# First attention of a language-model tower: value products of two key tiles issued as one group, and the rows of -1 of three key buffers written by POOL

## What is computed

```python
h = _L0_tok_ref(x, ...)                                  # token + position embedding
h = h + _L0_attn_ref(_layernorm(h), W_Q, W_K, W_V, W_O)  # this attention
h = h + _L0_ffn_ref(...); h = h + _L1_attn_ref(...); h = h + _L1_ffn_ref(...)

# inside _L0_attn_ref
scores = jnp.einsum('bhsd,bhtd->bhst', Q, K) / jnp.sqrt(jnp.float32(D_K))
scores = jnp.where(causal[None, None], scores, -jnp.inf)
attn = jax.nn.softmax(scores, axis=-1)
out = jnp.einsum('bhst,bhtd->bhsd', attn, V)
```

## Time and profile before

| | |
|---|---|
| median of 3 runs | 1530.04 us (1529.1 to 1531.93) |
| the profiled execution, device time | 1528.33 us |
| its span, first to last instruction | 1526.6 us |
| first attention (`attend_pairs`) in the span | from 117.4 to about 463 us |
| a step of it in the middle, TensorE | 10.3 us, 28 steps of this kind (u = 4 to 31) |
| a step at its end, without A (u = 32 to 34) | 7.19 us |
| mean granted clock of TensorE | 0.917 |

### The profile page before, as it was taken

One profiled execution on the slowest core, in us unless ns is written; L12 is line 12 of the kernel. 1 busy time (PEld: TensorE's weight loads), 2 busy tenths in 40 slices (PEclk: granted clock), 3 DMA queues, 4 the chain that ended last, 5 costly groups with the idle time before them and its releaser, 6 DMA issues. The chain is left out here.

```text
span 1526.6 us, 31400 instructions
## 1 busy us (share of the span) xinstructions
PE 1291.8 (85%) x10719; PEld 1003.0 (66%) x10720; DVE 855.6 (56%) x1797; ACT 662.8 (43%) x1260; POOL 633.0 (41%) x569
## 2 busy tenths in 40 slices
PE   6878999999996968980899566689959999989996
PEld 3655555555555847770667455589958888878886
DVE  5997776776744966996555355454423333323332
ACT  3871555555563644440344344233313343333332
POOL 7865665565004220777200000067213454444553
PEclk9995999999998997785899878799979999999998
DMA  1678877767400004654443311011036435454331
GB/s 52 199 254 266 265 228 247 231 223 230 115 4 15 1 5 137 183 178 127 91 110 85 110 42 47 10 28 28 29 129 213 116 51 133 127 132 130 52 55 19
DMA packets 122872, 179.38 MB, mean 118 GB/s; under 512 B 26052, under 2 KB 83820, under 8 KB 122772
## 3 DMA queue, kind: packets, MB, share of 16 engines
q1 hardware_dynamic: 94212, 117.15, 25.5%
q0 software_dynamic: 28560, 60.91, 15.2%
HBM read 104.73 MB, written 74.31 MB: 117 GB/s over the span
## 5 line engine op out<-in xcount | busy, mean ns | idle before, releaser
L1574 DVE TENSOR_REDUCE att_top<-att_psS 128x4 f32<-128x512 f32 (+2 forms) x192 | 195.9, 1036 | 80.6 <-PE att_psS L1458 80.6
L2725 POOL DMA_INDIRECT out<-ffn1c_y,ffn1c_table x72 | 113.9, 1582 | 177.1 <-ACT ffn1c_y L2838 99.3
L2866 DVE TENSOR_TENSOR ffn1c_hid<-ffn1c_psG,ffn1c_sil 128x512 f32<-128x512 f32 x72 | 49.8, 692 | 144.3 <-PE ffn1c_psG L2766 144.3
L1545 ACT ACTIVATE att_prob<-att_psS 128x1024 f32<-128x1024 f32 (+1 forms) x96 | 84.6, 883 | 92.0 <-PE att_psS L1478 91.9
L1545 ACT ACTIVATE pairs_part<-att_psS 128x1024 f32<-128x1024 f32 (+1 forms) x96 | 84.5, 883 | 67.0 <-PE att_psS L1478 66.7
L1452 PE MATMUL att_psS<-pairs_ka,pairs_qa 48*128 48x384 f32 (+3 forms) x512 | 107.3, 429 | 5.8 <-PEq L198 4.0
L1472 PE MATMUL att_psS<-pairs_qa,pairs_ka 50*128 50x256 f32 (+3 forms) x512 | 99.5, 401 | 12.2 <-DVE att_top L1574 12.0
L2766 PE MATMUL ffn1c_psG<-ffn1c_w_h,ffn1c_xh 128*128 x288 | 97.8, 422 | 11.3 <-DMA ffn1c_w_l<-experts_lo 3.9
L2714 POOL DMA_INDIRECT ffn1c_rows<-normed_rows,ffn1c_table x72 | 71.0, 986 | 78.4 <-DVE ffn1c_gate L2886 53.7
L1452 PEld LDWEIGHTS att_psS<-pairs_ka,pairs_qa 48*128 48x128 f32 x512 | 52.2, 200 | 70.4 <-issue 47.5
L2766 PE MATMUL ffn1c_psG<-ffn1c_w_l,ffn1c_xh 128*128 x288 | 90.9, 397 | 0.0
(11 more groups left out here) (413 smaller groups left out, 3605.2 us busy)
## 6 DMA issues: line engine op xcount, KB each, us to landing
prep_raw<-in_w_all POOLq DMA_DIRECT2D x27, 512.0 KB, 4.6
experts_hi<-prep_hi POOLq DMA_DIRECT2D x27, 512.0 KB, 3.8
experts_lo<-prep_lo POOLq DMA_DIRECT2D x27, 512.0 KB, 6.1
ffn1c_w_h<-experts_hi SPq DMA_DIRECT2D x8, 1536.0 KB, 6.6
ffn1c_w_l<-experts_lo SPq DMA_DIRECT2D x8, 1536.0 KB, 10.9
qkv_near<-near_keys SPq DMA_DIRECT2D x32, 320.0 KB, 4.3
q_parts<-pairs_part SPq DMA_DIRECT2D x8, 1024.0 KB, 4.1
k_parts<-pairs_part SPq DMA_DIRECT2D x16, 512.0 KB, 6.0
```

The lines of the kernel that those rows point to most:

```text
L1545: act.activation(dst, src, ACT.Exp, scale=0.25).then_inc(s["exp"], 1)
L1574: dve.tensor_reduce(dst, src, AX.X, ALU.max).then_inc(s["max"], 1)
L2725: pool.indirect_dma_start(out=rows_out, in_=y[:, t.buf, :], in_offset=None, out_offset=bass.IndirectOffsetOnAxis(ap=table[:, t.value:t.val ...
L2866: dve.tensor_tensor(hid[:, t.par, :], psG[:, t.par, 1, :], sil[:, t.par, :], ALU.mult).then_inc(s["act"], 1)
```

## The change

Two edits. In TensorE's walk, V0 moves from n = 4 to n = 5, directly ahead of V1, and V2 moves from n = 0 to n = 1, directly ahead of V3. The matmuls are the same. And the three memsets of key buffers 3 to 5 leave VectorE's steps 1 to 3; POOL issues them at the head of its part of `attend_pairs`, ahead of the first piece.

```diff
-    def dve_minus_rows(self, dve, at):
-        dve.memset(self.ka[:, at].bitcast(F32), -1.0).then_inc(self.s_minus, 1)
+    def minus_rows(self, eng, at):
+        eng.memset(self.ka[:, at].bitcast(F32), -1.0).then_inc(self.s_minus, 1)
...
             for at in range(pairs.EARLY):
-                pairs.dve_minus_rows(dve, at)
+                pairs.minus_rows(dve, at)
...
             piece, n_pieces = split
+            for at in range(pairs.EARLY, LOADED):
+                pairs.minus_rows(pool, at)
             for u in range(n_pieces):
...
-                    if n >= 4 and 0 <= u - 3 < NU:
-                        values(u - 3, n - 4)
-                    if n <= 1 and 0 <= u - 4 < NU:
-                        values(u - 4, n + 2)
+                    if n == 5 and 0 <= u - 3 < NU:
+                        values(u - 3, 0)
+                        values(u - 3, 1)
+                    if n == 1 and 0 <= u - 4 < NU:
+                        values(u - 4, 2)
+                        values(u - 4, 3)
...
             for u in range(NU + 4):
-                if pairs.EARLY <= u + AHEAD < LOADED:
-                    pairs.dve_minus_rows(dve, u + AHEAD)
                 for n in range(6):
```

## The result

The changed kernel took 1524.9 us (median of 8, 1520.96 to 1527.02), the kernel before 1530.8 in the same sessions: ratio 0.9957, 95% interval 0.9936 to 0.9978. So the two ratios say 0.4 and 0.2% faster, and both intervals leave out 1; 1526.5 had been forecast.

The account below looks back on a forecast made before the run. TensorE is 96% busy in the middle, but its step is partly a loop through DVE, which bounds the first steps. Steps 1.7, steps without A 1.0 and start 0.8 make 3.5 us: 1526.5 against 1530.04, 8-in-10 range 1522 to 1530.5.

Parts of the forecast that it names:

- The walk: Middle attention step followed row by row from A0 with spacings of the earlier trace: 10.24 us instead of 10.30.
- The two loops through VectorE: Middle step: B3 waits for the maximum of A2, and B5, in the new order, for that of A4.
- The 0.66 wait ahead of B5: Middle step: without V0 ahead of it, TensorE reaches B5 at 7.28 and waits for DVE until 7.94.
- the merges' 0.64: TensorE work removed per middle step: two merges at 0.32 each (entry 0.14, join 0.18); 18 us over 28 steps.
- The term of the steps, 1.7 us,: Middle steps: 0.06 us saved in each of 28 steps, 1.7 us; bounds 0 to 3.4.
- The steps without A, 1.0 us,: Steps 32 to 34: first merge worth nothing, second counts, 3 x 0.32 = 1.0 us; bounds nothing and 1.9.
- The start, 0.8 us,: First steps: 1.0 us from moving the memsets off DVE, less 0.2 for a later clock rise.
- The 0.2 taken off for a later rise: Start: V0 of unit 0 begins later, so the clock may rise later; costs 0.2 us, bounds 0 and 1.7.
- Rival 1: Whole kernel: no visible change, step keeps 10.30 and the start's gain is lost; 1528 to 1531 us, chance 0.31.
- Rival 2: Middle steps: merges won in full on TensorE, half being 9 us; 1511 to 1521 us, chance 0.05.
- Rival 3: Middle steps: clock falls because of waits at B3 and B5; ten steps at 1.2 GHz give 1550, chance 0.05.
- Rival 4: Middle steps: join not won, step 10.42 (1531.6 us) or 10.60 (1536.6 us); chance 0.05.

Follow-up runs that it names:

- e2: Changed kernel with only V2 and V3 merged, V0 back between B4 and A5, memsets on POOL; ratio 0.9930 to the kernel before.
- e3: Changed kernel with only V0 and V1 merged, V2 and V3 apart as before, memsets on POOL; ratio 1.0032 to the kernel before.
- e4: Changed kernel with merged V0 and V1 issued between A5 and B5 instead of behind B5; 1509.61 us, ratio 0.9846 to the kernel before.
- e7: Changed kernel with POOL's splitting of the expert weights started three steps later; ratio 0.9961 to the kernel before.
- e8: e4 and e7 together, against the changed kernel; 1509.06 us, ratio 0.9859 to the kernel before.
- e9: The changed kernel itself, nothing altered, timed again on a third chip; 1604.56 us, ratio 0.9980 to the kernel before.
- e10: The version of e4 timed again on the same chip as e9; 1586.03 us, ratio 0.9869 to the kernel before.
- e5: The kernel of e1 run again for a profile (memsets on POOL, value groups apart); no ratio on record, profile span 1525.8 us.
- e6: Changed kernel with merged value groups but the three memsets back on VectorE; ratio 0.9996 to the kernel before.
- e1: Changed kernel with the value groups apart as before, so only the memsets moved to POOL; ratio 0.9977 to the kernel before.

## Why the prediction was right

**The middle step.** The walk gave 10.24 and it measures 10.26; every anchor in it was within 0.02. The two loops through VectorE that it rested on are shown by e2, e3 and e4: each has its step from the same spacings, 9.90, 10.64 and 9.56 walked, 9.92, 10.64 and 9.60 measured. The 0.66 wait ahead of B5 was found as 0.62. Where the merges' 0.64 went is thus shown: the first merge brings B3 and the turn forward by 0.4, and V0, which had covered VectorE's time, now lies behind the wait and gives nearly all of it back. One spacing was read unlike the others: V3's 0.46 is busy time, and from its start to the next block it is 0.39 in the earlier trace rows. The join came out at 0.17 all the same, so this cost the forecast nothing.

**The term of the steps, 1.7 us,** was too large; it measured 0.5. A step gained 0.03, not 0.06, the difference of two numbers read to 0.01. That is 0.9 us in 27 steps, and a single step of 10.65 took 0.4 of them. In that step the maximum of A0 starts 1.19 after A0's weights instead of 0.81:

```profile
170.31 0.19 PEld L1454 LDWEIGHTS att_psS<-pairs_ka,pairs_qa 48*128 48x128 f32 x2 [0.60 <-issue]
...
171.50 1.82 DVE L1578 TENSOR_REDUCE att_top<-att_psS 128x4 f32<-128x512 f32 x2 [2.42 <-PE att_psS L1460]
```

The same 0.4 stands once in e2, e4, e7, e8, e9 and e10 and not in e3, e5 and e6: only with the memsets on POOL and V2 and V3 merged. No experiment went after its cause; it stays open.

**The steps without A, 1.0 us,** were 1.2. The prediction said that the first merge is worth nothing there, since the copy of the output waits for two exponentials anyway. But the second of the two had itself waited for B1, which stood behind V2. In the earlier trace rows the turn waits until 449.64, 3.39 after that step's B0; now it is 3.20 (444.13 to 447.33), the two exponentials taking 1.95 together where they took 2.13:

```profile
446.25 0.19 PEld L1472 LDWEIGHTS att_psS<-pairs_qa,pairs_ka 50*128 50x128 f32 x2 [0.59 <-ACT pairs_part L1545]
...
446.98 2.13 ACT L1545 ACTIVATE att_prob<-att_psS 128x1024 f32<-128x1024 f32 x2 [0.84 <-PE att_psS L1478]
```

So two steps gain 0.5 each and not 0.32. Of the other two of the four intervals from unit 27 to 31, the last gains 0.3 and the first loses 0.2 (8.01 to 8.18).

**The start, 0.8 us,** was 1.5, inside its bounds, but not by the reckoned way. The picture that only one memset would arrive, because A0 of step 3 waits for its key load, was wrong. That wait is there with the memsets on VectorE, 0.30 before and 1.46 in e6, and with them on POOL in e1 alone (0.22):

```profile
138.78 0.48 PE L1452 MATMUL att_psS<-pairs_ka,pairs_qa 48*128 48x128 f32 x2 [1.46 <-DMA pairs_ka<-k_parts]
```

What came late in the changed kernel's trace was the transfer of the maxima, 1.23 ahead of B0. By the transpose of unit 2's maxima the changed kernel had won 1.6 us (142.08 to 140.44), e5 without that wait 2.6 (to 139.47).

What halves the gain behind that is more likely the clock. From 112 us up to the rise at about 149 us TensorE runs at 1.2 GHz; a microsecond won before the rise is filled with work at half rate. If half the time of the rise is taken from the time of unit 0's turn, what is left is 82.0 for before and 81.4 for e6 (memsets on VectorE), 80.7 for e5 and 80.0 to 80.5 for the changed kernel and the five others with memsets on POOL. By that account the memsets are worth 0.9 to 1.3 and the merges of unit 0 another 0.2 to 0.6, and e5's transpose at 150.76 needs no other reason: 2.6 won ahead of it at half, and 3.2 of the rise at half. The account fits nine profiles; it isn't shown by an experiment that moved the rise by itself.

The 0.2 taken off for a later rise can't be seen in the changed kernel: V0 of unit 0 began at 147.18 and the clock rose at 149.1, against 147.14 and 149.0 before. But with the memsets in one place, the new order did begin V0 later and the rise came later: 144.53 and 145.8 in e5 against 147.18 and 149.1 in the changed kernel, 147.14 and 149.0 before against 149.29 and 152.8 in e6. About 1 us of each of these differences at V0 is a longer wait for a transfer. So this term was probably too small, and what the memsets won covered it. The rise came 0.9 to 3.5 us after the start of V0 in these nine profiles, too uneven for single profiles to give its size.

**The rivals.** Rival 1 (nothing to be seen) is close to what e6 gives by itself. Rival 2 is out: the merges were not won in full in this order, and two thirds of a microsecond a step more is what e4 wins by another. Rival 3: the clock stayed at 1.00 from 149 to 450 us, with both waits in every step. The rule that the prediction took from the Trainium skill (page "TensorE: Matmul & The Clock Gate", section "A second HAM failure mode: psum-queue depth-cycling"), that short idle times between groups make the clock swing, is not borne out by this trace, at idle times of 0.51 and 0.62 us ahead of B3 and B5. Rival 4: the join was won in the middle, V0 and V1 in 1.67 to the next block, where 1.02 and 0.82 apart make 1.84, and V2 and V3 in 0.82 (275.61 to 276.43), where 0.61 and 0.39 make 1.00.

**The forecast of the whole** lay at 3.5 us against 3.1 in the trace. That it came so near is partly luck: the term of the steps was 1.2 too large, those of the start and of the steps without A 0.7 and 0.2 too small, for separate reasons. The 6.6 us of the first ratio are not explained by the attention. From the next stage to the end, code that no kernel here changes took 1061.7 to 1066.9 us in the nine profiles of the table; this scatter is larger than the effect, and e9's 0.9980 is 3.2 us.

## What to carry to other kernels

In a ring of few buffers, an engine that is 96% busy can still be paced by another: walk one period from row to row, and look not at how long a piece of work is but at which wait it covers. In these runs, moving work that covered a wait to behind the wait lost (e3: less work, 0.35 a step longer); the same merge ahead of the waiting block took 0.66 off the changed kernel's step, 18.5 us in all (e9 and e10). When a merged group is to be placed, the place is found by the slack of each wait in the trace of before: here 0.50 at B5, covered by a V0 of 1.02.

## What the runs showed of the hardware

- Value products of successive key tiles in one group: each join saved 0.17 or 0.18 us (1.84 to 1.67 and 1.00 to 0.82), on top of 0.14 for the entry. Apart, a block of scores in the two halves of the array's rows stands between groups in four column tiles; that the change of tiles is what costs was not tested by itself.
- The clock rose between 145.8 and 152.8 us in nine profiles of nearly the same start, and in a tenth (e1) only at 636.7 us: there the step took 17.05 us instead of 10.29, and from 149 to 450 us the trace has PE busy 301 of 301 us at a granted clock of 0.50 (1.2 GHz).
- A POOL memset of 128x1024 f32 took 0.91 us (three in 2.73), the same as on VectorE.
- The transfer of the first maxima held PE for 1.23 us in one execution of the changed kernel and not at all in another (e9); over all profiles with the same work ahead of it, from nothing to 1.49 us (e10).
